# Linear attention of one layer: folded feature weights against projected keys and queries with row-half features

## What is computed

```python
def _relu_kernel(x, proj):                    # M = 128 features from DH = 64
    ratio = 1.0 / float(np.sqrt(proj.shape[0]))
    return jax.nn.relu(ratio * jnp.einsum('blhd,md->blhm', x, proj)) + EPS
q = jnp.einsum('bld,dhk->blhk', query_input, Wq)      # H = 16 heads, DH = 64
k = jnp.einsum('bld,dhk->blhk', source_input, Wk)
v = jnp.einsum('bld,dhk->blhk', source_input, Wv)
qp, kp = _relu_kernel(q, proj), _relu_kernel(k, proj)
kvs = jnp.einsum('blhm,blhd->bhmd', kp, v)
num = jnp.einsum('blhm,bhmd->blhd', qp, kvs)
den = jnp.einsum('blhm,bhm->blh', qp, jnp.sum(kp, axis=1))
return jnp.einsum('blhd,hdk->blk', num / den[..., None], Wo)
...
x = x + _L1_xattn_ref(_layernorm(x, axis=-1), ctx_1024, ...)
```

## Time and profile before

| what | value |
|---|---|
| median of 3 runs | 2972.48 us (2964.09 to 2979.94) |
| the profiled execution: its own time | 2989.71 us |
| the profiled execution: span | 2987.9 us |
| mean granted TensorE clock | 0.902 |
| PE busy | 2448.6 us, 82% |
| PE weight load busy | 1711.9 us, 57% |
| DVE busy | 1353.9 us, 45% |
| ACT busy | 1049.8 us, 35% |
| POOL busy | 827.4 us, 28% |
| third sub-block, layernorm starts | 578.6 us |
| fold starts | 594.1 us |
| main block, first matmul | 619.6 us |
| third sub-block, last instruction ends | 1298.1 us |

### The profile page before, as it was taken

One profiled execution on the slowest core, in us unless ns is written; L12 is line 12 of the kernel. 1 busy time (PEld: TensorE's weight loads), 2 busy tenths in 40 slices (PEclk: granted clock), 3 DMA queues, 4 the chain that ended last, 5 costly groups with the idle time before them and its releaser, 6 DMA issues. The chain is left out here.

```text
span 2987.9 us, 56361 instructions
## 1 busy us (share of the span) xinstructions
PE 2448.6 (82%) x20854; PEld 1711.9 (57%) x20854; DVE 1353.9 (45%) x3112; ACT 1049.8 (35%) x2183; POOL 827.4 (28%) x964
## 2 busy tenths in 40 slices
PE   4898579489999999969799999999856944999653
PEld 1555369467776776745456666666526832555442
DVE  3566401354555445544655555555541224455432
ACT  1455233243333233321255444454411201555311
POOL 3332110243344234300123223233241144222022
PEclk9899589799999999978899999999968976999767
DMA  5443089400000000000200000000015633322045
GB/s 166 98 105 73 16 287 328 152 11 12 12 12 8 11 12 7 2 1 22 77 17 13 8 13 13 12 13 2 5 36 183 212 107 74 71 71 60 2 141 155
DMA packets 167788, 195.56 MB, mean 65 GB/s; under 512 B 27512, under 2 KB 148224, under 8 KB 167552
## 3 DMA queue, kind: packets, MB, share of 16 engines
q1 hardware_dynamic: 157712, 166.52, 19.6%
q0 software_dynamic: 9840, 25.70, 2.6%
HBM read 141.93 MB, written 25.69 MB: 56 GB/s over the span
## 5 line engine op out<-in xcount | busy, mean ns | idle before, releaser
L811 DVE TENSOR_REDUCE a_mx<-a_s 112x2 f32<-112x750 f32 x256 | 234.5, 935 | 233.0 <-PE a_s L868 233.0
L1110 POOL TENSOR_TENSOR a_kp<-a_kp 125x512 f16<-125x512 f32 x192 | 218.9, 1158 | 400.4 <-ACT a_kp L1139 390.8
L1238 PE MATMUL a_u<-a_wkf,a_kc 128*125 128x512 f16 x1152 | 270.1, 396 | 26.1 <-issue 18.6
L305 POOL TENSOR_SCALAR a_P<-a_P,a_inv 112x375 f32<-112x375 f32 x256 | 148.4, 593 | 454.3 <-DVE a_inv L415 454.3
L1238 PEld LDWEIGHTS a_u<-a_wkf,a_kc 128*125 128x125 f16 x1152 | 161.5, 143 | 124.2 <-issue 41.1
L763 ACT ACTIVATE a_PT<-a_x 125x672 f32<-125x672 f32 x256 | 186.8, 730 | 104.0 <-PE a_x L881 102.5
L1160 DVE TENSOR_SCALAR a_kp<-a_u 125x512 f32<-125x512 f32 x192 | 128.5, 688 | 185.2 <-PE a_u L1238 154.9
L1933 ACT ACTIVATE f_h<-f_h,f_b1s 128x128 f32<-128x128 f32 (+1 forms) x294 | 116.3, 397 | 240.2 <-PE f_h L1907 227.5
L343 ACT ACTIVATE a_P<-a_masked,a_least 112x375 f32<-112x375 f32 x256 | 153.5, 600 | 100.6 <-DVE a_least L410 100.6
L1139 ACT CAST a_kp<-a_kp 125x512 f16<-125x512 f32 x192 | 117.7, 618 | 199.5 <-DVE a_kp L1160 199.4
L1907 PE MATMUL f_h<-f_xT,f_w 128*128 128x128 f32 (+1 forms) x1176 | 183.2, 312 | 0.1
(11 more groups left out here) (318 smaller groups left out, 4556.8 us busy)
## 6 DMA issues: line engine op xcount, KB each, us to landing
f_w<-in_L_ffn_W SPq DMA_DIRECT2D x42, 1024.0 KB, 6.6
a_kc<-in_ctxT SPq DMA_DIRECT2D x64, 375.0 KB, 3.9
f_w<-in_L_ffn_ew SPq DMA_DIRECT2D x42, 512.0 KB, 4.3
a_k<-a_k_parts SPq DMA_DIRECT2D x192, 93.8 KB
f_w<-in_L_ffn_W SPq DMA_DIRECT2D x42, 256.0 KB, 3.2
a_v_in_sb<-in_ctx SPq DMA_DIRECT2D x16, 375.0 KB
rows<-all_zero SPq DMA_DIRECT2D x6, 896.0 KB, 7.8
a_q<-a_q_parts SPq DMA_DIRECT2D x48, 112.0 KB, 3.8
```

The source lines that it names most:

```text
L305: pool.tensor_scalar(P[:, p % 4, r, :], P[:, p % 4, r, :], inv[:, p % 4, r:r + 1], 1.0, ALU.mult, ALU.mult).then_inc(P_done, 1)
L811: dve.tensor_reduce(mx[:, b % 2, 2 * pair:2 * pair + 2], s_bank[p % 2][0:S, :, 0:SK], AX.X, ALU.max).then_inc(max_done, 1)
L1110: pool.tensor_tensor(kp16[:, LO, j, w * 512:(w + 1) * 512], kp[:, n % 4, :], kp16[:, HI, j, w * 512:(w + 1) * 512], ALU.subtract).then_inc ...
L1238: mm = pe.matmul(out[0:KP, 0:512], kc16[:, u, a, c, j * KP:(j + 1) * KP], wt[:, z, c, w * 512:(w + 1) * 512], start=n_mm == 0, stop=n_mm = ...
```

## The change

The fold is gone. Wk, Wq, Wv and proj are split into half-precision parts; the split of Wk starts inside the layernorm through a new hook, `prepare_act`. Per batch PE makes eight "k" units (a projection of two heads each, 375 columns), and from these six "features" units; for two batches at once eight "q" units (224 columns) and four "qf" units (features of queries). ACT and DVE split k and q into halves. A features unit has 64 contraction rows, so the two heads of a projection lie in the two row halves of the array, and their matmuls alternate; it takes two banks of the ring, which has now five. kvs has one bank instead of two. The order is written in slots: 16 a batch, and unit kinds are placed by slot number `t` of their batch. The first ratio product of a batch is in slot 21 (slot 5 of the next batch), its divide in slot 22, the second ratio product in slot 24, its divide in slot 25, the output product in slot 28. There is no hardware loop: all 16 batches are written out.

```diff
-    units = [("k", j, n) for j in range(KT) for n in range(KN)] + \
-            [("v", j, n) for j in range(KT) for n in range(VN)] + [("q", g, 0) for g in range(H // 4)]
+    QB = 2
+    QW = QB * S
+    RING = 5
+    SLOTS = 16
+    FEATURES_AT = {5: (0, 0), 7: (0, 1), 9: (0, 2), 10: (1, 0), 12: (1, 1), 14: (1, 2)}
+    VALUES_AT = {8: (0, 0), 9: (1, 0), 11: (2, 0), 12: (0, 1), 13: (1, 1), 15: (2, 1)}
+            found += [("sums", b, t - 18)] if 18 <= t <= 21 else []
+            found += [("ratio", b, 0)] if t == 21 else [("ratio", b, 1)] if t == 24 else []
+            found += [("out", b, 0)] if t == 28 else []
+            found += [("k", b, t)] if 0 <= t < C else []
+            found += [("features", b, FEATURES_AT[t])] if t in FEATURES_AT else []
+            found += [("v", b, VALUES_AT[t])] if t in VALUES_AT else []
+            if b % QB == 0:
+                found += [("q", b // QB, (t - 1) // 2)] if 1 <= t < 17 and t % 2 == 1 else []
+                found += [("qf", b // QB, (t - 6) // 4)] if t in (6, 10, 14, 18) else []
...
+        def prepare_act(act):
+            act.wait_ge(wk_in, 16)
+            act.mul(wk16[:, HI, :, :], staged[:, 0, :, :], WS).then_inc(wk_hi, 1)
...
@@ scalar @@
+                for s in steps:
+                    if s >= 1:
+                        for unit in units_at(s - 1):
+                            if unit[0] == "features":
+                                high_features(unit)
+                    for unit in units_at(s):
+                        if unit[0] in ("k", "q", "v", "sums"):
+                            evacuate(unit)
...
@@ vector @@
+                for s in steps:
+                    for unit in units_at(s):
+                        if unit[0] in ("k", "q", "v", "features", "qf"):
+                            take(unit)
+                    for b in range(B):
+                        t = s - SLOTS * b
+                        if t in (22, 25):
+                            divide(b, (t - 22) // 3)
+                        if t == 29:
+                            add_out(b)
...
@@ tensor @@
+                    elif kind == "features":
+                        hf, j = c
+                        pe.wait_ge(pp_split, 1)
+                        outs = claim(unit)
+                        taken(pe, ("k", b, 4 * hf + 3))
+                        for i in range(4):
+                            for n, (x, z) in enumerate(PARTS):
+                                for r in range(2):
+                                    mm = pe.matmul(outs[r][0:KP, i * M:(i + 1) * M],
+                                                   k16[64 * r:64 * r + DH, x, 4 * hf + i, j * KP:(j + 1) * KP],
+                                                   pp16[64 * r:64 * r + DH, z, :], start=n == 0, stop=n == 2)
+                        mm.then_inc(projected["features"], 1)
...
+                def ratio(b, hf):
+                    g, t = divmod(b, QB)
                     pe.wait_ge(kvs_evac, 4 * b + 2 * hf + 2)
+                    taken(pe, ("qf", g, 2 * hf + 1), 1)
+                    if 2 * b + hf >= 1:
                         pe.wait_ge(att_done, 2 * b + hf)
```

More of the change, by code:

```diff
@@ L156, in _ @@
                                    bias=eps[:, 0:1]).then_inc(std_done, 1)
+                if prepare_act is not None:
+                    prepare_act(act)
                 for g in range(G):
@@ L1072, in linear_attention_phase @@
[L1072 to L1085 removed]
+        attT = m.sb("attT", [128, C, S])
@@ L1087, in linear_attention_phase @@
+        p_bank = [m.bank(f"p{i}") for i in range(RING)]
+        kvs_bank, num_bank, den_bank = m.bank("kvs_sum"), m.bank("num"), m.bank("den")
         with nc.Block() as block:
@@ L1114, in body @@
-                def body(b, u):
-                    for n in range(NK):
-                        feature_low(b, u, n)
-                    if not last(b):
-                        low(b + 1, 1 - u)
-                low(0, 0)
-                bodies(pool, body)
+                for s in steps:
+                    for unit in units_at(s):
+                        if unit[0] == "features":
+                            low_features(unit)
+                    if s % SLOTS == 4 and s // SLOTS + 1 < B:
+                        split_context(s // SLOTS + 1)
@@ new lines, in high_features @@
+                def high_features(unit):
+                    _, b, (hf, j) = unit
+                    if b >= 1:
+                        act.wait_ge(summed, 4 * (b - 1) + 2 * hf + 2)
+                    for r in range(2):
+                        n = 2 * feats[unit] + r
+                        act.wait_ge(f_evac, n + 1)
+                        act.copy(kp16[:, HI, j, hf, r, :, :].rearrange("p c m -> p (c m)"), kp[:, n % 4, :]).then_inc(f_hi, 1)
+                high_context(0)
+                act.wait_ge(rest_in, 48)
@@ L1264, in num_den, with claim, three @@
-                def num_den(b, u, hf):
+                def claim(unit):
+                    for earlier, r in before[unit]:
+                        taken(pe, earlier, r)
+                    return [p_bank[bank] for bank in place[unit]]
+                def three(out, lhs, rhs, mm=None):
+                    for i, (x, z) in enumerate(PARTS):
+                        for j in range(DC):
+                            mm = pe.matmul(out, lhs(x, z, j), rhs(x, z, j), start=i == j == 0, stop=(i, j) == (2, DC - 1))
+                    return mm
@@ new lines, in sums @@
+                def sums(b, g):
+                    hf = g // 2
+                    pe.wait_ge(f_low, 2 * feats["features", b, (hf, 2)] + 2)
+                    taken(pe, ("v", b, (2, hf)))
+                    if b == g == 0:
+                        pe.wait_ge(ones_made, 2)
+                    if 4 * b + g >= 1:
+                        pe.wait_ge(kvs_evac, 4 * b + g)
+                    for hh in range(4):
+                        h = 4 * g + hh
+                        c, r = divmod(h, 2)
+                        n = 0
+                        for x, z in PARTS:
+                            for j in range(KT):
+                                mm = pe.matmul(kvs_bank[:, hh * VC:(hh + 1) * VC], kp16[:, x, j, hf, r, c % 4, :],
+                                               v16[:, z, j, h, :], start=n == 0, stop=n == 3 * KT - 1)
+                                n += 1
+                    mm.then_inc(summed, 1)
```

510 lines of the change are left out of this document (242 added, 268 removed).

## The result

The changed kernel takes **3008.57 us** (median of 4 runs, 2999.26 to 3014.7), the kernel before 2976.21 beside it: a ratio of **1.0108** (95% interval 1.0075 to 1.014). The forecast was 2999 us, and slower by 0.9%.

What follows compares the result with a forecast made beforehand. PE sets the time, with room on the other engines. Terms of -23 - 66 - 32 + 104 + 41 + 2 = +26 us on the profiled 2989.7 give 3015.7; the median lies 17.2 lower, so 2999 us, range 2900 to 3050.

Steps and rivals of the forecast that it cites:

- likeliest case: Main block: PE waits for the divides and loses a part of the clock, 2999 us; chance 0.50.
- Ahead of the loop: Start of the main block: first matmul comes earlier without the fold, -23 us; bounds up to 5 us less gain.
- PE work: PE's units in each batch: 16.2 us added in place of 20.3 gone, -4.1 a batch, -66 us for 16.
- Loop: Loop over batches: written out, six returns of 3.2 us idle and 2.1 us slow clock go, -32 us.
- The waits: Second ratio product and output product: PE stands for the divides, 6.9 us a batch in 15 batches, +104 us.
- The bottom rival: Main block: the divides are hidden and only the gains are left, -119 us, 2853 us; chance 0.24.
- Clock: PE behind the waits: 2.1 us of slow clock at 6 or 7 in 10 of them, +41 us; bounds 0 and 81.
- The rival in which it holds: Main block: the waits are there but PE stays at 2.4 GHz, 2958 us; chance 0.20.
- Tail: End of the sub-block: with one kvs bank the last key sums wait for their copies, 3 x 0.6 us, +2.
- The sign: Whole kernel, told from no change at 0.5%: slower 0.56, within 0.20, faster 0.24.
- deciding number: PE's idle plus lost clock per batch: under 7.9 us the change gains.

Runs made afterwards that it cites:

- experiment 1: The changed kernel with the reciprocal left out, attT formed from num alone: 2878.41 us, 0.9622 of the kernel before.
- Experiment 11: The changed kernel with the 12 matmuls of one row half ahead of the 12 of the other in a features unit: 3054.38 us, a single run.
- experiment 2: The kernel before with its loop over 16 batches written out, nothing else: 2946.37 us, 0.9868 of the kernel before.
- experiment 4: The changed kernel with 14 and 12 useless matmuls put into two of PE's waits: 2977.08 us, 0.9994 of the kernel before.
- experiment 5: The changed kernel with ACT taking its own slot's units ahead of the features' roundings: 3007.12 us, 1.0063 of the kernel before.

## Why the prediction was right, point by point

The forecast of 2999 us lies 0.3% from the 3008.57 measured, and its likeliest case happened. Its sum was +26 us for the profiled execution; the sub-block grew by 22.2, and the medians moved by 32.4. That it is as near as 0.3% is partly luck. For two batches of the steady state, what the steps said and what was measured (work from experiment 1, waits from the time line above with one of 0.28, clock as the rest of the 89.4):

| us per two batches | predicted | measured |
|---|---|---|
| PE work | 71.2 | 73.2 |
| waits | 13.8 | 12.0 |
| clock | 5.4 | 4.2 |
| together | 90.4 | 89.4 |

- **Ahead of the loop** (-23): -22.2, counted from the start of the layernorm. The high part of Wk was free, as assumed. The first matmul came at 3.95 us behind the cast and not at 2.64, within the bound of 5: POOL's low part of the context took 2.89 us while DVE split Wk.
- **PE work** (-4.1 a batch) was mis-sized: it is -3.1. The features unit has a pitch of 0.84, close to the 0.79 taken. What was missing is what the change of row halves costs the unit ahead of it: a k unit ahead of features takes 1.07 us (898.02 to 899.09), where 0.98 had been read in the earlier trace rows, and a v unit 1.44 (912.32 to 913.76) where 1.30 had been read in the earlier trace rows. A batch has eight such units, six ahead of features and two ahead of qf; at 0.1 each that is 0.8 of the 1.0. The prediction had put this price into the features unit itself, 0.14. Experiment 11 leaves little of it there: 24 matmuls one after the other are 24 x 0.054 = 1.30 of the 1.36 measured, so most of the surplus in the 0.84 (12 x 0.054 = 0.65) goes with taking turns. The weight loads are no limit: 24 loads and matmuls in 0.84 us, 0.035 each.
- **Loop** (-32): -32.0 in the main block by experiment 2, -35.8 by the medians. No cost of straight code showed.
- **The waits** (6.9 a batch) were right in place, releaser and order: 3.88 for the 4.4 foretold, 2.66 for 3.0, 2.88 for 3.3, 2.27 for 2.5, each 0.2 to 0.5 short. They come to 6.0. For the first, with zero at 898.02: PE reaches it at 4.8 and not at 4.5, since its own units took longer, and leaves it at 8.7 and not at 8.9, since the hand-overs are shorter. So the missing work and the surplus of waits are in part one and the same error: what PE works longer ahead of a divide, it waits less. DVE was busy for 26 us a batch and not for 29: it waits for ACT's halves in between, and it is the order that makes PE stand. The bottom rival (divides hidden, 2853) is refuted, and experiment 1 shows that its arithmetic was sound: without the reciprocal it is 2878, and of the 25 us above 2853 the larger work is 16 and the waits that are left (1.17 a pair) are 9.
- **Clock** (+41): some 32 by the table (4.2 for each of 7.5 pairs), 23 to 31 by experiment 4, which left a wait unfilled. The rival in which it holds is refuted: the stretches show 0.94 to 0.97. It was the softest term, and stays so: in experiment 5 it moved against the waits, and why is open.
- **Tail** (+2): the last key sums wait 2.4 us for their copies (1.31, 0.56 and 0.56).

The errors, +2.0 in work and -3.0 in waits and clock a pair, partly cancel; so the total is nearer than the terms are. The sign was a close thing: the prediction's deciding number, idle and lost clock of PE under 7.9 us a batch for a gain, came out at 6.0 + 2.1 = 8.1. With the work as measured (-3.1 a batch, so 6.9 in place of 7.9) the margin is wider.

## What to carry to other kernels

Count the work that PE has between a product and the product that waits for its post-processing: making that work cheaper (here from 7.8 us to 4.8) exposes the chain on the other engine, and the saved time comes back as idle and again as lost clock. Here such waits were cured by order, without a faster divide: move the waiting product back, split the long instruction so that the ring's tiles pass between its halves, and only then polish the order on the feeding engine (3.4 us of the main block before the others, 16 behind them). Compare a rewrite with the cheapest fix of the old form too: writing out the loop alone was worth 1.3%.

## What the runs showed that I had not expected

- Useless work made the kernel faster: 12 or 14 matmuls in each place where PE stood longest took it from 3008.57 to 2977.08 us, with 23 us less in the main block, at a clock of 0.99 to 1.00.
- A shorter wait need not save time: in experiment 5, 1.5 us less idle a pair came with 0.01 to 0.03 less clock.
- An elementwise POOL instruction of 750 columns took 2.89 us beside a DVE instruction of 2048 columns; the median of its 16 is 1.56. DVE's ended at 587.71, 1.42 us behind POOL's start, and 1.42 + 1.56 is 2.98: as if POOL had waited for its end. It is one event, and no run tests it.
- A unit of full rows costs PE about 0.1 us more when a unit in row halves follows: a k unit 1.07 us against the 0.98 of the earlier trace rows, and the last v unit ahead of features 1.44 against 1.34 ahead of a q unit (866.78 to 868.12).
